# A graph attention layer with three source tiles rounded instead of one, their small products on parts that a transfer makes

## The reference

```python
def gat_layer(x, W, att_src, att_dst, bias, src, dst, heads, out_ch, concat):
    h = (x @ W.T).reshape(n, heads, out_ch)
    e = leaky_relu(a_src[src] + a_dst[dst], 0.2)
    m = segment_max(e, dst)
    ex = exp(e - m[dst])
    alpha = ex / (segment_sum(ex, dst)[dst] + 1e-16)
    return segment_sum(alpha[:, :, None] * h[src], dst) + bias
...
x = x + gat_layer(relu(gat_layer(layernorm(x), W1, 8 heads x 128)), W2, 1 head x 768)
x = x + ffn(layernorm(x))       # 6 class tokens by routed experts, the rest by fc1, gelu, fc2
```

## Time and profile before

| what | us |
|---|---|
| runs (median; lowest to highest) | 714.18 (713.35 to 715.71) |
| profiled execution, device time | 713.25 |
| its span, first to last instruction | 711.4 |
| TensorE busy | 701.1 (99%) |
| VectorE busy | 529.0 (74%) |
| ScalarE busy | 420.0 (59%) |
| GpSimd busy | 114.1 (16%) |

### The profile page before, as it was taken

One profiled execution on the slowest core, in us unless ns is written; L12 is line 12 of the kernel. 1 busy time (PEld: TensorE's weight loads), 2 busy tenths in 40 slices (PEclk: granted clock), 3 DMA queues, 4 the chain that ended last, 5 costly groups with the idle time before them and its releaser, 6 DMA issues.

```text
span 711.4 us, 13502 instructions
## 1 busy us (share of the span) xinstructions
PE 701.1 (99%) x4670; PEld 657.9 (92%) x4670; DVE 529.0 (74%) x878; ACT 420.0 (59%) x863; POOL 114.1 (16%) x95
## 2 busy tenths in 40 slices
PE   8899999999999999999999999999999999999997
PEld 6699999889899999999999999999999899999997
DVE  5999888698899999999999664445568752737232
ACT  4665584388688888888888754454443333522202
POOL 2559421000000000000000000000223331222202
PEclk9999999999999999999999999999999999999999
DMA  8727888645314131322310443201881734315102
GB/s 279 223 68 195 262 244 232 174 140 163 95 40 114 31 102 55 94 67 64 102 32 22 109 111 67 62 0 36 247 282 49 222 91 189 100 58 177 44 23 67
DMA packets 53362, 84.10 MB, mean 118 GB/s; under 512 B 15081, under 2 KB 36399, under 8 KB 53312
## 3 DMA queue, kind: packets, MB, share of 16 engines
q1 hardware_dynamic: 47628, 65.69, 32.6%
q10 hardware_dynamic: 4500, 13.82, 6.0%
q0 software_dynamic: 1184, 3.92, 1.9%
HBM read 68.09 MB, written 15.33 MB: 117 GB/s over the span
## 4 chain that ended last, share of the span: by engine, by line
PE 91%; DMA 4%; DVE 3%; issue 0%; POOL 0%; ACT 0%; ACTq 0%; SPq 0%; DVEq 0%
PE bank L1426 22%; PE bank L1571 13%; PE bank L1402 12%; PE bank L1498 12%; PE bank L1298 11%; PE bank L1675 4%; DMA w1n_sb<-in_W 3%; PE bank L1647 3%; PE bank L1213 3%; PE bank L1552 2%; PE bank L1701 1%; DVE x2f L2312 1%; PE bank L1215 1%; PE bank L1228 1%; PE bank L1732 1%; DVE fc_lo L2279 1%
## 5 line engine op out<-in xcount | busy, mean ns | idle before, releaser
L1426 PE MATMUL bank<-PT,h1s 125*128 125x250 f32 x730 | 161.0, 374 | 0.0
L1426 PEld LDWEIGHTS bank<-PT,h1s 125*128 125x128 f32 x730 | 135.3, 190 | 14.4
L2078 DVE SCALAR_TENSOR_TENSOR L<-asb,nadh 125x1250 f32<-125x1250 f32 x80 | 117.9, 1515 | 1.9 <-PE bank L1402 0.9
L2087 DVE CUSTOM_DVE_ANT_0 L<-L,LC 125x1250 f32<-125x1250 f32 x80 | 113.4, 1454 | 0.6 <-DMA LC<-log_count_scratch 0.4
L914 ACT ACTIVATE L<-L,nm 125x1250 f32<-125x1250 f32 x80 | 108.4, 1384 | 2.7 <-DVE nm L2087 1.9
L932 ACT COPY PT<-bank 125x500 f32<-125x500 f32 x165 | 87.4, 613 | 35.9 <-PE bank L1402 35.9
L1402 PE MATMUL bank<-ident,L 125*125 125x125 f32 x800 | 94.2, 273 | 0.0
L1402 PEld LDWEIGHTS bank<-ident,L 125*125 125x125 f32 x800 | 91.2, 189 | 0.9 <-issue 0.4
L1884 DVE TENSOR_TENSOR hotr<-iota,r 125x1500 f16<-125x1500 f16 x50 | 46.5, 931 | 7.8 <-PE bank L1215 4.2
L743 POOL MEMSET pick<- 128x90 f32 x1 | 0.2, 168 | 267.2 <-ACT hT L965 267.2
L1571 PE MATMUL bank<-h_hi,PT_hi 125*125 125x384 f32 x200 | 41.5, 350 | 0.0
(11 more groups left out here) (285 smaller groups left out, 1353.9 us busy)
## 6 DMA issues: line engine op xcount, KB each, us to landing
asb<-src_logit_rows SPq DMA_DIRECT2D x28, 312.5 KB, 3.9
atom_w<-in_atom_inT SPq DMA_DIRECT2D x5, 1152.0 KB, 12.5
atom_w<-in_atom_outT SPq DMA_DIRECT2D x5, 1152.0 KB, 9.4
log_count_scratch<-LCw SPq DMA_DIRECT2D x10, 546.9 KB
LC<-log_count_scratch SPq DMA_DIRECT2D x10, 546.9 KB
LCt<-log_count_scratch SPq DMA_DIRECT2D x10, 546.9 KB
h_scratch<-h1st ACTq DMA_DIRECT2D x10, 448.0 KB
rdT<-reciprocal_scratch SPq DMA_DIRECT2D x8, 500.0 KB, 4.6
```

The source lines that it names most:

```text
L1426: mm = pe.matmul(sums, h1s[q][:, s, :], PT[p][:, s, :], start=(s == 0), stop=(plain and s == NT - 1))
L2078: dve.scalar_tensor_tensor(L[r][:, :], asb[q][0:NP, 1, :], nadh[q][:, t:t + 1], asb[q][0:NP, 0, :], ALU.add, ALU.max).then_inc(stt_done, 1)
L2087: dve.tensor_tensor_reduce(out=L[r][:, :], in0=L[r][:, :], in1=LC[:, t, :], scale=-1.0, scalar=-FLOOR, op0=ALU.add, op1=ALU.min, accum_out ...
```

## The change

`RING` = 5 tiles of exponentials instead of four, and VectorE works one tile ahead: `blocks(k)` gives the tiles 2k + 1 and 2k + 2 in step k instead of 2k and 2k + 1. The logit instruction takes its target logit from `nad1` with the head's register as index; the copy `nadh` is gone. `exp` is called once per tile, the first of the two before `evac`.

Source tiles 0, 1 and 2 are rounded (`PART` = 0; bank 0 holds tiles 0 and 1, bank 1 tiles 2 and 3). ScalarE writes the rounded high halves of all three in `PT_hi` (tile 2 negated) and the exact values of tiles 1 and 2 in `PT` (tile 1 negated). VectorE makes the low half of tile 0 alone, as before. The low halves of tiles 1 and 2 are made by two transfers that GpSimd issues for each pair: one copies the exact values to `PT_sum`, one adds the rounded ones to it. Two products read `PT_sum`, in the next step, between the transposes of bank 3 and of bank 4. The other seven rounded products end `aggregate`. GpSimd also makes the low halves of the features once a head, and ScalarE their high halves, plain and negated.

`rrow` is a single tile now, so ScalarE waits for the store before (`rden_stored`). W2 is one load after the weights of layer two's logits, which move from k = 6, 7 to k = 3, 4. `asb` comes in three pieces. The scratch tensors of the loop lie elsewhere in memory. The first head stays plain.

```diff
-QUARTERS = 4
-PART = 2
+TURNED_BANKS = NG * NG * H
+PIECES = [0, 834, 1667, 2500]
+RING = 5
+PART = 0
...
+            def lower_by_sum(hh, kk):
+                n, p = 2 * NG * hh + kk, kk % 2
+                if kk % NG == 0:
+                    q = kk // NG % 2
+                    pool.wait_ge(features_high, 2 * hh + kk // NG)
+                    alone(pool)
+                    pool.tensor_tensor(h1p_lo[q][:, 0:2, :], h1s[q][:, 0:2, :], h1p_hi[q][:, 0:2, :].bitcast(F32),
+                                       ALU.subtract)
+                    pool.tensor_tensor(h1p_lo[q][:, 2, :], h1p_hi[q][:, 2, :].bitcast(F32), h1s[q][:, 2, :],
+                                       ALU.subtract).then_inc(features_lower, 1)
+                pool.wait_ge(tb_evac, NG * n + 2)
+                if not isinstance(n, int) or n > NG + 1:
+                    pool.wait_ge(sums_done, n + -(NG + 1))
+                alone(pool)
+                pool.dma_start(PT_sum[p][:, :, :].bitcast(F32), PT[p][:, 1:3, :]).then_inc(raw_moved, 16)
+                pool.wait_ge(raw_moved, 16 * n + (16 - 16 * NG))
+                alone(pool)
+                pool.dma_start(PT_sum[p][:, :, :].bitcast(F32), PT_hi[p][:, 1:3, :].bitcast(F32), accum_op=ALU.add
+                               ).then_inc(lower_moved[p], 16)
...
                     if b == 0 and not (first and k - lag < 2):
                         act.wait_ge(agg_done, n + -1)
+                        if not (first and k - 3 < NG):
+                            act.wait_ge(lower_moved[(k - 3) % 2], moved(hh, k - 3))
...
                     if b == PART // 2 and not (first and k - lag < NG):
-                        act.copy(PT_hi[(k - lag) % 2][:, :], turned[0:NP, 0:GW])
-                        act.copy(PT[(k - lag) % 2][:, PART + 1, :], turned[0:NP, GW:2 * GW]).then_inc(tb_evac, 1)
+                        act.copy(PT_hi[(k - lag) % 2][:, 0:2, :],
+                                 turned[0:NP, 0:2 * GW].rearrange("p (s n) -> p s n", s=2))
+                        act.activation(PT[(k - lag) % 2][:, 1, :], turned[0:NP, GW:2 * GW], ACT.Copy, scale=-1.0
+                                       ).then_inc(tb_evac, 1)
+                    elif b == 1 and not (first and k - lag < NG):
+                        act.copy(PT[(k - lag) % 2][:, 2:4, :],
+                                 turned[0:NP, 0:2 * GW].rearrange("p (s n) -> p s n", s=2))
+                        act.activation(PT_hi[(k - lag) % 2][:, 2, :], turned[0:NP, 0:GW], ACT.Copy, scale=-1.0
+                                       ).then_inc(tb_evac, 1)
...
             def step(hh, k, **at_end):
                 ahead = at_end.get("first") and k in (1, 2)
+                exp(hh, k, 0, **at_end)
                 if ahead:
-                    exp(hh, k, **at_end)
+                    exp(hh, k, 1, **at_end)
                 evac(hh, k, **at_end)
                 if not ahead:
-                    exp(hh, k, **at_end)
+                    exp(hh, k, 1, **at_end)
...
-                    pe.matmul(sums, h1p[q][:, 0, :], PT_hi[p][:, :], start=False, stop=False)
-                    pe.matmul(sums, h1p[q][:, 1, :], PT_hi[p][:, :], start=False, stop=False)
-                    mm = pe.matmul(sums, h1p[q][:, 0, :], PT_lo[p][:, :], start=False, stop=True)
+                    for s in range(3):
+                        high = h1p_neg[q][:, 1, :] if s == 2 else h1p_hi[q][:, s, :]
+                        pe.matmul(sums, high, PT_hi[p][:, s, :], start=False, stop=False)
+                        pe.matmul(sums, h1p_lo[q][:, s, :], PT_hi[p][:, s, :], start=False, stop=False)
+                    mm = pe.matmul(sums, h1p_hi[q][:, 0, :], PT_lo[p][:, :], start=False, stop=False)
                 mm.then_inc(agg_done, 1)
+            def moved_parts(hh, k, first=False, last=False):
+                lag = 3
...
+                pe.wait_ge(lower_moved[p], moved(hh, k - lag))
+                pe.matmul(sums, h1p_neg[q][:, 0, :], PT_sum[p][:, 0, :], start=False, stop=False)
+                pe.matmul(sums, h1p_hi[q][:, 2, :], PT_sum[p][:, 1, :], start=False, stop=True).then_inc(sums_done, 1)
...
             def step(hh, k, **at_end):
-                for b in range(5):
+                for b in range(4):
                     turn_bank(hh, k, b, **at_end)
+                moved_parts(hh, k, **at_end)
+                turn_bank(hh, k, 4, **at_end)
                 turn_reciprocals(hh, k, **at_end)
                 aggregate(hh, k, **at_end)
...
+                        dve.scalar_tensor_tensor(L[s % RING][:, :], asb[q][0:NP, 1, :],
+                                                 nad1[:, ds(h, 1), t:t + 1].rearrange("p h t -> p (h t)"),
+                                                 asb[q][0:NP, 0, :], ALU.add, ALU.max).then_inc(stt_done, 1)
```

235 lines of the change are left out of this document (132 added, 103 removed).

## The result

The changed kernel takes 717.2 us (median; 715.02 to 720.99) against 714.19 (713.05 to 715.94) for the kernel before, run beside it: ratio 1.0054, interval [1.0040, 1.0068]. It is slower: by 3.0 us between these two medians, by 3.9 us if the ratio is applied to 714.19. The forecast was 709.4, faster. The profiled execution has a span of 715.4 us, 4.0 more than the 711.4 of before.

The account below looks back on a forecast made before the run. TensorE was taken as the bound, in an unbroken chain: 713.25 - 5.1 (loop) - 0.2 (last reciprocals) + 0.5 (tail) = 708.5 us profiled, 709.4 as median of runs; range 708.0 to 730.0.

Parts of the forecast that it names:

- The product prices: TensorE, attention loop: plain source tile 0.423 us, rounded product 0.117 us; step falls from 6.34 to 6.20 us.
- Rival 4: Loop: rounded products between the transposes cost 0.18 us extra, so no time gained; 714 to 716 us; chance 0.10.
- The gain of 5.1 us: TensorE, attention loop: 0.145 us saved in each of 35 steps that use rounding, 5.1 us in all.
- The tail: Loop's end: the last pair's transfers have only the last products as cover; 0.5 us of loss put there.
- The margin of 3.0 us in the loop: Loop: a pair's two transfers land at 9.9 us, wanted at 12.9 and later, so they stay hidden.
- Rival 3: Transfers are the bound, through slow adding or feature loads and logit rows lying across; 712 to 722 us; chance 0.14.
- GpSimd's subtractions: Once a head, features' lower parts: 0.6 and 0.3 us plus some start, about 1.0 us together.
- rival 2: VectorE locks out GpSimd's subtractions, delaying transfers once a head: 724 to 733 us, chance 0.20; 750 or more, chance 0.08.
- VectorE: Loop: slack 1.3 us in ten steps against 2.0 us if it gives way to GpSimd; lag costs 0 to 0.5 us.
- ScalarE: Loop: 5.95 us a step plus 0.08, under the 6.20 us period, so it costs nothing, with thin cover.
- The 0.2 us at the last reciprocals: Loop's end: VectorE's subtraction can run earlier, so TensorE's wait for the last reciprocals goes; up to 0.2 us gained.
- The sign: Whole kernel: forecast faster, chance 0.50; within no change 0.16; slower 0.34.

Follow-up runs that it names:

- e1: Changed kernel with layer two's reciprocal-row loads cut to one head of eight (62 KB instead of 500 KB each; different result); 711.63 us, ratio 0.9961.
- e5: Changed kernel with the last head's last two pairs plain and without transfers, as in the kernel before; 711.81 us, ratio 0.9987.
- e2: Changed kernel with GpSimd's two subtractions per head replaced by a zero fill, leaving out features' low parts; 715.87 us, ratio 1.0022.
- e7: Changed kernel with GpSimd's subtractions done twice per head, the first time into unread memory; 737.54 us, ratio 1.0248.
- e8: Changed kernel with VectorE computing the reciprocals in a step's first block, ahead of the second block's logits; 727.71 us, ratio 1.0196.
- e6: e5 with VectorE computing the reciprocals in a step's first block, ahead of the second block's logits; 716.69 us, ratio 1.0053.
- e11: Changed kernel with the features' lower parts subtracted on VectorE instead of GpSimd; 717.91 us, ratio 1.0057.
- e10: e5 with the features' lower parts subtracted on VectorE instead of GpSimd; 711.87 us, ratio 0.9984.
- e9: e7 with all the doubled subtractions behind the issue of the pair's plain copy, ahead of the wait for its landing; 723.59 us, ratio 1.0127.
- e4: Changed kernel with only the last products reordered: last pair's products ahead of the moved pair of the pair before; one execution, 725.19 us.
- e12: Changed kernel with layer two's reciprocal-row loads after the first held back from the last pairs' transfers; 715.04 us, ratio 1.0023.

## Why the prediction was wrong, point by point

**The product prices: right.** Plain products 0.423, rounded 0.12, the moved pair 0.25 for two: the step is 6.19 to 6.31 us as forecast. Rival 4 (0.18 more for the moved pair) is refuted by the row at 285.45. The gain of 5.1 us was there as TensorE's work, step by step; 4.8 of it belong to the 33 steps, of which 2.9 reached the time.

**The tail: the step that failed.** The term of the sum for the transfers at the loop's end was "I put 0.5 us there"; it is 7.1. That is 6.6 of the 8.7 us between the forecast for the profiled execution, 708.5, and its 717.2, and alone enough to turn the sign. The transfers' prices were right where nothing lies beside them: 4.0 us for the copy and 4.4 for the adding one, by the page's medians, against 3.8 assumed, and the adding one is hardly longer. Three things were missed. First, I named the reciprocals' loads in half a sentence and gave them no price; copies that lie beside them land after 7.1 and 8.4 us. Second, I counted the last pair's transfers alone. The pair before it is hit too, and since GpSimd issues in order its lateness is handed on: the pair before the last has its adding transfer leave at 400.53, and only then goes the last copy, at 401.16. Third, I had no term for the clock: 1.7 us of the 7.1. e1 and e5 show the collision from either side. The size of 7.1 is that of one profile; other kernels with the same end lose from 4.1 us on (e2).

**The margin of 3.0 us in the loop: held**, at GpSimd's landing times; TensorE does not wait for a transfer between 200 and 390 us in the changed kernel. Rival 3, with a chance of 0.14, was the nearest in substance (transfers bound by loads that lie across, 712 to 722), but I placed it in the loop, once a head, with feature loads and logit rows.

**GpSimd's subtractions: rival 2 was right that they can push the transfers until TensorE stands, and wrong in how and when.** I priced them at 0.6 and 0.3 us; they take 1.03 to 1.56 and 1.66 to 2.06, always with VectorE at work beside them. They are not locked out until VectorE pauses, as the rival had it, so "one a step" did not happen. I said that it decides as soon as the second ends later than 5.2 us into the step. That point was too early: it ended at 5.5 in e7 and 6.4 in e8 without a pause, and from 6.8 on (e6, e7, e8) TensorE stood. The changed kernel has 4.6 at most, and TensorE stands nowhere for it. What stood in for the lock was the length of the work and its place in the queue.

**VectorE: the second miss, and a smaller one.** I allowed for 2.0 us in ten steps with the start of both; 2 x 0.77 = 1.5 were held. I allowed 0 to 0.5 us for the lag and put nothing into the sum; e2 gives back 0.9. The remaining 1.0 us of the 1.9 missing in 33 steps is about what steps 11, 21 and 31, in which reciprocals lie, are too long in e2; that they are long by VectorE's fixed work is read from the chain of one of them, and no run takes that work away. I counted the slack of VectorE as a sum over ten steps, while it is short within one. e11 and e10 do not settle it further: 207.35 and 206.75 in 33 steps, which is no more than the profiles differ.

**ScalarE: right.** 185.06 us in 190 is 6.1 a step, forecast 5.95 + 0.08. Its cover was as thin as stated: at step 21 its copies end the wait.

**The sum.** With the measured stages it reads 713.25 - 2.9 + 7.1 - 0.3 = 717.15, the 717.2 of the profiled execution; that it closes is arithmetic, since the stages are cut from these two profiles. The 0.2 us at the last reciprocals was gained as forecast: TensorE no longer stands there. The range, to 730, held the time, but it was drawn that wide for rival 2, which did not happen here. The sign was missed: slower had a chance of 0.34, and for another reason.

## What to carry to other kernels

A chain of transfers that is hidden in a loop must be priced again at the loop's end, with every load that the next phase issues there; a collision at that place costs the pauses and, behind them, the clock. When a queue is in order, compute for each item the latest time at which the items behind it still keep their deadline: subtractions of 3 us led to no pause where they ended up to 6.4 us into the step, and to one of 2.3 to 3.8 us, in most cases with the lower clock during or behind it, where they ended at 6.8 or later (e6, e7, e8). Work that can fill a wait belongs behind the issue whose landing is waited for, not ahead of it (e9 against e7: 8.6 us).

## What the runs showed of the hardware

- A pause of TensorE of 2.81 us in after was followed by 3.4 us at the 1.2 GHz level, from 0.9 us after work was taken up again. In the pause of 3.02 us of e8 (231.4 to 234.4) the clock fell at 233.4, and stayed low for 6.8 us. In the pause of 7.43 us of e4 the clock fell 3 us after the pause had begun and stayed low for 10.2 us. In e12 three pauses of 1.42, 0.88 and 1.06 us within 11 us had 3.4 us of it behind them. The second pause of after, 2.59 us, both pauses of e2, 1.33 and 2.72 us, and a pause of 0.53 us in e1 had none, while a first pause of 1.98 us in e11 had 3.4 us behind it. So the length of a pause alone did not decide.
- A transfer of 244 KB inside SBUF lands after 4.0 us, the adding one after 4.4, with 0.55 and 0.84 us of GpSimd to issue them. Beside two broadcast loads of 500 KB each the copy lands after 7.1 and 8.4 us, and the first two loads take 7.5 and 9.4 where they took 4.9 and 6.5 before.
- GpSimd subtracts 256 columns in 1.0 to 1.6 us and 128 columns in 1.7 to 2.1 beside VectorE's maxima and logits: the second one is longer with half the columns. VectorE does them in 0.42 and 0.29 (GpSimd's rows overlap each other in places, as at 216.44, so its durations are rough). The Trainium skill, page "SBUF — State Buffer", section "Who interferes with whom", says that a VectorE instruction with two SBUF inputs and a GpSimd instruction that reads SBUF exclude each other for a whole instruction. The maxima of 2.55 and 1.69 us where 1.45 is usual and the stretched subtractions agree in that each side waits for the other; that GpSimd finds no way in until VectorE pauses, the rival that I made of it, did not happen here.
